# Cross-attention block with an audio block behind it: context pieces and masks issued by GpSimd, key transposes moved between a tile's high and low transposes

## What is computed

```python
# L0: two cross-attention layers and an MLP over x (8, 56, 256), context (8, 1500, 256), 16 heads of 128
x = x + cross_attention(layer_norm(x), ctx, ...)      # twice
x = x + gelu(layer_norm(x) @ w_fc1 + b_fc1) @ w_fc2 + b_fc2
# L1, the audio block: 16 heads of 16
a = layer_norm(audio_kv)                              # audio_kv is the same context
Q = (hidden_states @ Wq.T) ; K = (a @ Wk.T) ; V = (a @ Wv.T)      # reshaped to heads
scores = jnp.where(mask, einsum('bhtd,bhsd->bhts', Q, K) * scale, -inf)
out = einsum('bhts,bhsd->bhtd', softmax(scores), V) @ Wo.T
return hidden_states + jnp.tanh(gate) * out
```

## Time and profile before

| | us |
|---|---|
| Median of the runs | 1482.26 |
| Lowest and highest of the 3 runs | 1479.71 and 1484.2 |
| The profiled execution | 1483.11 |
| Its span, first to last instruction | 1481.2 |

### The profile page before, as it was taken

One profiled execution on the slowest core, in us unless ns is written; L12 is line 12 of the kernel. 1 busy time (PEld: TensorE's weight loads), 2 busy tenths in 40 slices (PEclk: granted clock), 3 DMA queues, 4 the chain that ended last, 5 costly groups with the idle time before them and its releaser, 6 DMA issues.

```text
span 1481.2 us, 24729 instructions
## 1 busy us (share of the span) xinstructions
PE 1419.8 (96%) x9188; PEld 891.6 (60%) x9188; DVE 983.6 (66%) x2034; ACT 867.0 (59%) x1564; POOL 469.7 (32%) x379
## 2 busy tenths in 40 slices
PE   8899999999999999999999999999899899999987
PEld 5466666666666654466666666666554455555555
DVE  6665555555556657676566566665557888888886
ACT  5655445544555446545544555445445698888987
POOL 3534425334334200144433433430002333333300
PEclk9999999999999999999999999999999999999999
DMA  5299899898899730398889889988721699999998
GB/s 198 64 228 191 163 185 183 161 187 180 173 177 179 157 102 29 88 205 187 177 171 181 184 164 180 187 164 155 172 58 37 133 218 218 213 210 220 219 201 167
DMA packets 672083, 246.95 MB, mean 167 GB/s; under 512 B 644716, under 2 KB 646236, under 8 KB 671964
## 3 DMA queue, kind: packets, MB, share of 16 engines
q1 hardware_dynamic: 671964, 245.38, 81.6%
HBM read 85.28 MB, written 0.52 MB: 58 GB/s over the span
## 4 chain that ended last, share of the span: by engine, by line
PE 73%; DVE 8%; DMA 7%; ACT 5%; SPq 3%; issue 2%; ACTq 0%; DVEq 0%
PE SC L755 40%; PE PV L755 33%; DMA core<-qc 4%; DVE qc L1538 2%; ACT qc L1278 2%; DVE prob L1520 1%; DMA qc<-core 1%; DVE core L1579 1%; DMA core<-core 1%; ACT prob L1269 1%; SPq L550 1%; ACT core L1262 1%; DVE core L1571 1%; DVE core L1419 1%; DMA core<-in_wv_dram 1%
## 5 line engine op out<-in xcount | busy, mean ns | idle before, releaser
L755 PE MATMUL PV<-core 128*128 128x256 f16 (+1 forms) x4800 | 542.1, 271 | 16.6 <-DMA core<-qc 7.4
L755 PEld LDWEIGHTS PV<-core 128*128 128x128 f16 x4800 | 458.7, 98 | 88.7 <-issue 15.1
L1211 ACT ACTIVATE prob<-SC,core 128x500 f32<-128x500 f32 x336 | 223.8, 674 | 419.5 <-DVE core L1544 419.5
L755 PE MATMUL SC<-ctxT,qc 128*128 128x500 f16 x2016 | 445.4, 375 | 0.0
L1513 DVE TENSOR_REDUCE mx<-SC 128x1 f32<-128x500 f32 x336 | 224.9, 670 | 331.9 <-PE SC L755 331.9
L755 PEld LDWEIGHTS SC<-ctxT,qc 128*128 128x128 f16 x2016 | 196.2, 97 | 208.2 <-issue 1.9
L683 POOL CAST ctxT<-stage 128x750 f16<-128x750 f32 x64 | 69.3, 1083 | 454.9 <-PE SC L755 239.3
L1571 DVE SCALAR_TENSOR_TENSOR core<-prob,core 128x1500 f16<-128x1500 f32 x112 | 194.4, 1736 | 4.3 <-ACT core L1220 4.3
L1220 ACT ACTIVATE core<-prob 128x1500 f16<-128x1500 f32 x112 | 162.7, 1453 | 3.6
L755 PE MATMUL SC<-ctxT 128*128 128x512 f16 x576 | 137.1, 381 | 8.4 <-DVE core L1579 8.3
L755 PE MATMUL SC<-qc 128*128 128x512 f16 x480 | 113.5, 381 | 11.7 <-DVE mx L1520 11.7
(11 more groups left out here) (135 smaller groups left out, 1321.5 us busy)
## 6 DMA issues: line engine op xcount, KB each, us to landing
stage<-in_ctx_nat_dram SPq DMA_DIRECT2D x64, 384.0 KB, 3.9
stage<-in_ctx_t_dram SPq DMA_DIRECT2D x64, 375.0 KB, 3.4
stage<-in_ctx_p_dram SPq DMA_DIRECT2D x32, 384.0 KB, 3.9
core<-in_wq_dram SPq DMA_DIRECT2D x8, 512.0 KB, 3.7
core<-in_wk_dram SPq DMA_DIRECT2D x8, 512.0 KB, 3.6
core<-in_wv_dram SPq DMA_DIRECT2D x8, 512.0 KB, 5.1
core<-in_wo_dram SPq DMA_DIRECT2D x8, 512.0 KB, 5.2
core<-core SPq DMA_TRANSPOSE x224, 4.1
```

The lines of the kernel that those rows point to most:

```text
L755: return nc.tensor.matmul(o, a, c, start=start, stop=stop, skip_group_check=skip)
L1211: nc.scalar.activation(prob[:, i, c * CW:c * CW + w], SETS[i][c][:, 0:w], ACT.Exp, bias=nmax[:, i, :], accum_out=sum3[:, i, c:c + 1]).then ...
```

## The change

Three things are written in another way.

1. The context pieces of batches 2 to 7 of the audio block are issued by GpSimd and not by SyncE. GpSimd issues piece k of batch b+1 at the end of `split_audio(b, k)`, right after its own subtraction has finished, on a semaphore of its own for each buffer (`audio_full`). The pieces of batches 0 and 1 stay with SyncE.
2. All eight `mask_load` calls are GpSimd's: one ahead of the first `split_audio`, the others at the head of each batch of GpSimd's loop, ahead of `spread_queries`.
3. SyncE's `turn_audio` is cut into `turn_high` and `turn_low`, and a key transpose stands between the two, where it stood ahead of both.

```diff
@@ sync @@
-            def turn_audio(y):
+            def turn_high(y):
...
                 sp.dma_start_transpose(probT[:, 0:NT, s * P:(s + 1) * P], aph[:, i, 0:TC]).then_inc(apth_full[i], 16)
+
+            def turn_low(y):
+
+                s, i = y % RT, y % 2
                 sp.wait_ge(aph_lo, y + 1)
...
-            mask_load(0)
...
             for y in range(RT * B + 1):
                 b, s = divmod(y, RT)
+                if y > 0:
+                    turn_high(y - 1)
                 if s in SLOT_KEYS and b + 1 < B:
                     turn_keys(PIECES * (b + 1) + SLOT_KEYS[s])
                 if y > 0:
-                    turn_audio(y - 1)
-                if s < PIECES and b + 2 < B:
-                    piece(2, b + 2, s, False)
-                if s == 1 and b + 1 < B:
-                    mask_load(b + 1)
+                    turn_low(y - 1)
@@ gpsimd @@
-                pool.wait_ge(stage_full[k], 16 * slot_uses(2, b, False))
-                if b >= 2:
+                if b < 2:
+                    pool.wait_ge(stage_full[k], 16 * slot_uses(2, b, False))
+                else:
+                    pool.wait_ge(audio_full[k], 16 * (b - 1))
                     between_tiles(RT * (b - 2) + 2 + k)
...
                 nc.gpsimd.tensor_tensor(lo, stage[:, k, :], hi, ALU.subtract).then_inc(stage_free, 1)
+                if 1 <= b < B - 1:
+                    pool.wait_ge(stage_free, 16 * B + PIECES * b + k + 1)
+                    pool.dma_start(stage[:, k, :], ctx_p[b + 1, :, k * DC * PW:(k + 1) * DC * PW])\
+                        .then_inc(audio_full[k], 16)
...
+            mask_load(0)
             for k in range(PIECES):
                 split_audio(0, k)
...
             for b in range(B):
                 if b + 1 < B:
+                    mask_load(b + 1)
                     pool.wait_ge(pad_ready, 1)
                     spread_queries(b + 1)
```

More of the change, by code:

```diff
@@ L263, in build @@
         mask_full = sem("mask_full")
+        audio_full = [sem(f"audio_full{k}") for k in range(PIECES)]
         mask_ready = sem("mask_ready")
@@ L495, in token_row @@
                                  tok_hl[part * H:(part + 1) * H, i, b * Q:(b + 1) * Q]).then_inc(tokrow_full[b % 2], 16)
[L497 to L500, removed]
             def turn_probs(t):
@@ L707, in split_audio, with mask_load @@
                 nc.gpsimd.tensor_tensor(lo, stage[:, k, :], hi, ALU.subtract).then_inc(stage_free, 1)
+                if 1 <= b < B - 1:
+                    pool.wait_ge(stage_free, 16 * B + PIECES * b + k + 1)
+                    pool.dma_start(stage[:, k, :], ctx_p[b + 1, :, k * DC * PW:(k + 1) * DC * PW])\
+                        .then_inc(audio_full[k], 16)
+            def mask_load(b):
+                if b > 0:
+                    pool.wait_ge(mask_ready, b)
+                pool.dma_start(mask8[:, :], mask[b:b + 1, :].broadcast_to([P, T])).then_inc(mask_full, 16)
             def spread_queries(b):
```

## The result

The changed kernel takes 1488.71 us in the median of 8 runs (1485.82 to 1497.89), the kernel before 1481.64 beside it (1479.71 to 1486.08). The ratio is 1.0054, 95% interval [1.0032, 1.0075]: slower, and above the range of 1466 to 1488. The profiled execution took 1487.42 us; it is read against the 1483.11 us of the one before.

A forecast was written before the change was run, and what follows sets the result against it. SyncE's queue was taken as the bound of audio batches 1 to 5; relieved, each falls from 40.96 to 39.3 us, 8.3 in all, so 1482.26 - 8.3 gives 1474 us, range 1470 to 1478, 8 in 10 from 1466 to 1488.

The forecast's parts named there:

- The bound: Audio block, batches 1 to 5: SyncE's queue fills the period, 41.23 us in batch 3 with next to no gap.
- The price of a piece from a second queue: What a GpSimd piece costs SyncE's transposes: 1.2 us, taken between 0.58 and 1.75.
- The 38.8 us for the queue: SyncE's need per batch after the change: 33.4 for transposes, 4 x 1.2 for pieces, 0.6 for the mask.
- The engines' need: An undisturbed audio batch: 28.6 us for slots 0 to 4 plus 10.7 for slots 5 and 6, together 39.3.
- It falls below what the other engines need together: SyncE's queue at 38.8 us a batch drops under the other engines' 39.3, gaining 8.3 us over five batches.
- The key at slot 5: Key transpose issued behind the high one, at 1313.80 instead of 1311.97; covered with a queue 2 to 3 us behind, booked at 0.
- The mask: Mask loads moved to GpSimd: 8 issues, one in a batch, asked for a batch early, so nobody waits.
- being wrong from the start: Sign against the whole prediction: the attention stages, whose code is untouched, come out different.
- The landing of a piece: A context piece lands within 4.7 us of its issue at worst and is wanted a whole batch later.
- High transposes: At slots 0, 2, 4 and 5 they go out 1.85 us earlier, meeting ScalarE's 12.9 us of waits; nothing beyond the 8.3.
- The slower one: Rival: GpSimd's pieces meet key transposes at slots 2 to 5, each costing over about 1.75 us; 1492 us, chance 0.18.
- The engines are the bound: Rival: a piece takes 1.75 us from the transposes whoever issues it, the period stays; 1479 to 1484 us, chance 0.25.

The follow-up runs named there:

- e4: The changed kernel without the requests for the pieces of batches 2 to 7, which compute on what batch 1 left; 1469.05 us, 0.9912.
- e13: The changed kernel word for word, timed again in five rounds; 1491.36 us, 1.0059 against the kernel before.
- e9: The changed kernel with its pieces of batches 3 to 7 issued by SyncE at slots 2 to 5, masks still GpSimd's; 1484.75 us, 0.9997.
- e14: The changed kernel with the key transpose at slot 5 put back ahead of the high one; 1485.75 us, 1.0030.
- e1: The kernel before with the order high, key, low alone; pieces and masks stay on SyncE; 1482.58 us, 1.0009.
- e3: The kernel before with only the masks issued by GpSimd; 1481.83 us, 1.0000.
- e7: The kernel before with its first mask moved behind the weights in SyncE's program; 1480.98 us, 0.9979.
- e15: e9 with the key at slot 5 ahead of the high transpose and all masks from SyncE, the first behind the weights; 1478.57 us, 0.9976.
- e16: e15 with all four key transposes ahead of the high ones, as in the kernel before; 1479.50 us, 0.9976.
- e2: The changed kernel with the old order key, high, low; pieces and masks from GpSimd; 1482.76 us, 1.0010.
- e5: The changed kernel with GpSimd requesting piece k at slot k (0 to 3) and the mask at slot 1; 1481.09 us, 0.9989.
- e17: e15 with the pieces of batches 2 to 7 requested by GpSimd, masks still SyncE's; 1484.26 us, 1.0007.
- e18: e17 with every piece requested in two halves, one straight behind the other; 1482.49 us, 0.9988.
- e10: The changed kernel with all masks given back to SyncE, the first behind the weights; 1486.62 us, 1.0010.
- e11: e5 with all masks given back to SyncE; 1486.81 us, 1.0004.
- e12: The changed kernel word for word, one execution; 1486.06 us, where the kernel before had 1484.66.
- e6: The changed kernel with GpSimd requesting two pieces at slot 6, one with the mask at slot 1, one at slot 3; 1493.00 us, 1.0057.

## Why the prediction was wrong, step by step

**The bound.** Right: SyncE's queue, 39.1 us of issues and 1.6 of short gaps in batches of 40.96, and without pieces 33.7 in 38.9.

**The price of a piece from a second queue** was well sized in the mean: 1.2 us forecast, 1.5, 1.2 and 1.1 in the three profiles. The 38.8 us for the queue was not. It adds 33.4 for the transposes, counted from start to start where five stood in a row, and 0.6 for the mask, 34.0; e4 needs 35.2 for the two. With the pieces the queue needs 41.4, 39.9 and 39.5 us in batches 1 to 4 of the three profiles.

**The engines' need.** 39.3 forecast, 38.9 in e4. Right.

**"It falls below what the other engines need together"** is the step that failed, in two ways. First, it does not fall below: the engines need 38.9 (e4) and the queue 39.5 to 41.4. In batches 1, 2 and 4 of the first profile it is still the bound, with 0.95 us of long gaps in all three, and they take 41.3 us in the mean where the same three took 41.0 before. Second, even the 38.8 against 39.3 left half a us in a batch of seven tiles, and I treated two means as if the smaller could hide behind the larger. The price does not come evenly. Most transposes are issued in 1.4 to 2.9 us, and in a few batches one or two take 4 to 6. `aph` has two buffers and TensorE's averages wait for the newest tile. My reading is that nothing carries 4 us of lateness over: behind the long ones SyncE stands still at other slots (8.5 us of gaps over 0.3 us in batches 1 to 5, of which 4.77 in batch 3, against 0.4 before) and cannot give it back. More buffers were not tried. After the longest idle times the clock takes 1 to 2 us more, 3.2 in batch 3 as a whole.

**The key at slot 5**, "with a queue 2 to 3 us behind it is covered. I book this part at 0": wrong too. The text had worked out that it lands too late in a queue as late as now; it was 9.0 us of waits in the changed kernel, 12.5 in e13 and 10.2 in e9. Putting it back took 5.6 us off the median (e14 against e13; the intervals overlap), and batch 0 is some 2 us or more shorter in every profile that has it ahead. With pieces at slots 0 to 3 the same order costs no time that can be told (e1).

**The mask**, booked at nothing, is nothing in sum (e3, 1.0000), but of two parts that I saw neither of. The audio block starts some 4 us earlier. The two profiles are level within 1 us until 1051 and part at the end of the attention, whose change I had named as a sign of being wrong from the start; it comes from the place of the first mask (e7). And batches 1 to 5 take 41.7 us each in e3's profile against 40.96, slot 0 of batches 1 and 2 8.5 each against 7.1 and 7.8. GpSimd is not shown to be the reason for the second: e7, whose masks SyncE issues, has 41.5.

**The landing of a piece**, within 4.7 us of its issue at worst from SyncE, takes up to 10.4 us from GpSimd. Nobody waits for it, as forecast, since it is wanted a batch later. GpSimd's 0.55 us for an issue are hidden, as forecast too.

**High transposes.** Right: ScalarE's 12.9 us went. It was worth nothing (e1, and e15 against e16), since ScalarE's waits moved between 12.9, 10.4 and 4.4 us with no time to show for it.

**The rivals.** The slower one named the right places, slots 5 and 6 and the first scores of a batch, and both of its marks are in the profile. Its 1492 is 3 us off the measured time. But its condition, a piece above 1.75 us, is not what happened: a mean of 1.3, and 1.5 at most, was enough. So its number is near by luck, and its chance of 0.18 was set by the wrong quantity. "The engines are the bound" holds for the sum over a batch, and its sign is in the profile too: transposes around GpSimd's pieces take about 3 us and more, and batches 2 and 4 have no long gap. It would have said 1479 to 1484, which is nearly where the kernels with the pieces at SyncE are (1478.6 to 1484.8), and those of GpSimd in which the requests or the order stand otherwise (e2, e5, e17, e18: 1481.1 to 1484.3).

**How far each part is shown.** That GpSimd's pieces go with long single transposes in the audio block is shown by eleven profiles against nine. That they cost time by themselves is not shown against the kernel before: e2, e5, e10, e11, e17 and e18 request all pieces from GpSimd and are not apart from it. What is shown is that the changed kernel, with requests at slots 2 to 5, masks with them and the key of slot 5 behind, loses half a per cent, twice. For the issuer by itself the nearest pair is e9 against the changed kernel, which have order, places and masks in common: 0.9997 against 1.0054 and 1.0059, intervals that do not meet, but on three chips, and on e9's own the one execution of the changed kernel (e12) is 1.3 us above e9's median. Then there are e17 against e15 (0.3%, two chips) and e13 and e14 against e15 and e16 (0.8 and 0.5% on one chip, with the masks in the difference and for e13 the key). Why it holds them up stays open: neither the mask (e10) nor halved requests (e18) made an end of it.

The fastest version seen that does all the work is e15, 1478.57 us or 0.24% under the kernel before. Its batches are no shorter than before (41.1 against 40.96 us), it starts the audio block at 1153.1, and e7, which moves the first mask alone, has the same ratio within the interval. The places of SyncE's pieces contribute nothing that these runs could tell; those of GpSimd's do (e5 against the changed kernel).

## What to carry to other kernels

Before you call a queue relieved, add up its issues and the gaps between them over the stretches that do the work, and leave out those that don't: the batch without pieces hid 1.1 us of issues a batch here. When a queue and the engines behind it need nearly the same time per period, ask not only for the mean of what is moved but for its longest single delay, and count the buffers between it and the engine that waits. Here work taken away counted (e4, 0.9912), and work handed to another issuer did not. A transfer whose consumer opens the next period should stay ahead of those that have a step to spare. Time a change of this kind in several executions and more than one profile: one long batch, 6.2 us, is nearly the 7.1 us between the two medians.

## What was not expected of the hardware

- A copy of 384 KB requested by GpSimd beside DMA transposes was issued in 0.55 us and landed in 4.5 us in the median and 10.4 at most, against 0.58 to 0.87, 3.9 and 4.7 from SyncE. It cost the transposes about as much in the mean (1.1 to 1.5 us, against 1.2), but single ones took up to 6.74 us to issue, while in the two worst places the DMA share stood over 1 and the rate fell to 81 and 114 GB/s.
- Behind two such requests one after the other a transpose took 6.36 us to issue (e6).
- After 5.51 us of idleness 12 matmuls took 2.42 us and not 1.31, at a granted clock of 0.71 in that stretch; after 2.75 us of idleness 12 others took 4.44 and not 2.75, at 0.75.
- A mask of 188 KB requested ahead of weights in the same queue goes with a wait of 8.5 to 8.7 us for those weights, in three profiles of three.
- The spread of single runs grew with GpSimd's requests: 1475.2 to 1483.7 us in e16, 1480.2 to 1499.0 in the changed kernel on the same chip.
